# Graph layer with residual and layer norm: a ring of 24 chunks instead of 84, and one 192-wide sum per chunk instead of one 496-wide sum per three chunks

## What is computed

```
h_self   = x @ W_self.T + b_self
messages = x[src] @ W_neigh.T + b_neigh
h_neigh  = segment_sum(messages, dst, 50000)
y        = x + relu(h_self + h_neigh)
out      = (y - mean(y)) / sqrt(var(y) + 1e-5)      # per node
```

## Time and profile before

| | us |
|---|---|
| median of 3 runs (lowest to highest) | 804.39 (798.32 to 804.57) |
| the profiled execution | 803.84 |
| its span, first to last instruction | 802.0 |
| busy: PE / DVE / ACT / POOL | 557.8 / 446.4 / 303.2 / 403.5 |

### The profile page before, as it was taken

The page is one execution under the profiler, slowest core; times in us unless marked ns, Lnnn a source line. Parts: engine busy times, 40 slices in busy tenths (PEclk is TensorE's granted clock), DMA queues, the critical chain, the costliest instruction groups (busy, mean ns, idle before and its releaser), DMA issues. The chain is left out here.

```text
span 802.0 us, 11397 instructions
## 1 busy us (share of the span) xinstructions
PE 557.8 (70%) x3151; PEld 441.7 (55%) x3151; DVE 446.4 (56%) x1927; ACT 303.2 (38%) x789; POOL 403.5 (50%) x424
## 2 busy tenths in 40 slices
PE   2054011069742979888678886978897988999995
PEld 0033001048631767666557675756675776778784
DVE  8880100048812777776566757565554555566765
ACT  0000000025311535444234544535453544566566
POOL 5777777520375656660756666556565666100000
PEclk9998555559955989998879999889997999999998
DMA  2421211123312434453334443444444444433433
GB/s 76 120 56 52 62 52 52 43 60 101 104 52 63 127 113 128 132 150 95 102 93 134 123 133 110 123 114 132 115 136 112 131 123 134 119 105 101 116 104 93
DMA packets 122933, 82.12 MB, mean 102 GB/s; under 512 B 15374, under 2 KB 115894, under 8 KB 122840
## 3 DMA queue, kind: packets, MB, share of 16 engines
q1 hardware_dynamic: 109208, 53.63, 23.7%
q0 software_dynamic: 13664, 27.77, 12.9%
HBM read 55.44 MB, written 26.71 MB: 102 GB/s over the span
## 5 line engine op out<-in xcount | busy, mean ns | idle before, releaser
L467 POOL DMA_INDIRECT ring<-in_x,chunk_src x391 | 378.7, 968 | 271.7 <-issue 110.9
L994 ACT COPY sums_t<-bank 128x496 f32 x131 | 74.8, 571 | 423.9 <-remote 202.2
L893 PE MATMUL bank<-pick,ring 128*128 128x192 f32 (+2 forms) x782 | 231.9, 437 | 4.0 <-DMA ring<-in_x,chunk_src 4.0
L739 DVE SCALAR_TENSOR_TENSOR y<-bank,x_in 128x384 f32<-128x384 f32 x131 | 72.6, 554 | 215.7 <-remote 173.2
L912 PE MATMUL bank<-wsum_t,x_t 128*128 128x128 f32 (+1 forms) x782 | 175.4, 307 | 15.2 <-issue 15.2
L913 PE MATMUL bank<-wn_t,sums_t 128*128 128x128 f32 (+1 forms) x782 | 160.8, 287 | 24.2 <-issue 24.2
L1021 ACT ACTIVATE result<-y,minus_mean,rstd 128x128 f32<-128x128 f32 x391 | 163.4, 486 | 0.0
L893 PEld LDWEIGHTS bank<-pick,ring 128*128 128x128 f32 x782 | 146.1, 210 | 19.0 <-issue 4.3
L912 PEld LDWEIGHTS bank<-wsum_t,x_t 128*128 128x128 f32 (+1 forms) x782 | 126.6, 203 | 40.0 <-issue 39.8
L913 PEld LDWEIGHTS bank<-wn_t,sums_t 128*128 128x128 f32 (+1 forms) x782 | 127.6, 204 | 24.8 <-issue 24.8
L887 PE MATMUL bank<-carry,ring 128*128 128x1 f32 x260 | 44.6, 241 | 106.8 <-DVE pick L728 77.8
(11 more groups left out here) (122 smaller groups left out, 207.9 us busy)
## 6 DMA issues: line engine op xcount, KB each, us to landing
x_in<-in_x SPq DMA_DIRECT2D x130, 192.0 KB
out<-result SPq DMA_DIRECT2D x130, 192.0 KB
ring<-in_x,chunk_src POOLq DMA_INDIRECT x391
degrees_t<-degrees_dram SPq DMA_DIRECT2D x130, 2.2 KB
dst_padded<-in_dst SPq DMA_DIRECT2D x1, 390.6 KB
src_padded<-in_src SPq DMA_DIRECT2D x1, 390.6 KB
edge_src<-in_src SPq DMA_DIRECT2D x1, 390.6 KB
edge_dst<-in_dst SPq DMA_DIRECT2D x1, 390.6 KB
```

The lines of the kernel that those rows point to most:

```text
L467: nc.gpsimd.indirect_dma_start(ring[:, c % RING, :], None, x, bass.IndirectOffsetOnAxis(ap=chunk_src[:, c:c + 1], axis=0)).then_inc(gather ...
L739: v.scalar_tensor_tensor(y[tau % DEEP][0:rows, 0:tiles, :], h_bank[b][0:rows, 0:tiles * DIM].rearrange("p (q d) -> p q d", q=tiles), 0.0, ...
L893: ins = mm(sums[:, lo:hi], ring[:, c % RING, :], pick[tau % DEEP][:, PICK_AT[q]:PICK_AT[q] + hi - lo], start=(tau == 0 and q == 0), stop=( ...
L994: nc.scalar.copy(sums_t[:, bass.ds(at, SPAN)], sum_bank[tau % SUM_BANKS][:, 0:SPAN]).then_inc(sums_placed, 1)
```

## The change

Two things are changed at once.

**The ring** has 24 slots instead of 84, and POOL waits for each chunk by itself (`chunks_summed`) and no longer for triples.

**The sums** are made chunk by chunk. Each chunk covers 192 columns counted from its own first node; two chunks stand side by side in one bank, at columns 0 and 192. The pick of the first of a pair is 193 columns wide: its last column adds the edges that belong to the second's first node. The second's own overhang goes into column 0 of the next pair's bank by a `carry` matmul, so there is one carry matmul for two chunks. ACT copies 192 columns per chunk, each copy waiting for the one before, with one wait on the sums for a pair. Registers are loaded eight at a time. There are four sum banks, and one bank for the turned `x`. The margin that is joined at a lap's end is 192 columns wide instead of 512, and the drift allowed is 640 nodes instead of 768 (384 within 42 chunks of either end, 192 within 9). How far the sums run ahead is now counted in chunks: what is needed, plus 2, rounded up to a whole pair.

```diff
-SPANS = ((0, 192), (64, 344), (168, 496))
-SPAN = SPANS[-1][1]
-PICK_AT = (0, 192, 472)
-PICK = 800
+SPAN = 192
+PAIR = 2
...
-MARGIN = 512
+MARGIN = SPAN
-DRIFT = 768
+DRIFT = 640
...
-RING = 84
+RING = 24
-SUM_BANKS = 3
-LOAD = 4
+SUM_BANKS = 4
+LOAD = 8
...
+def chunks_starting_below(node):
+    return 1 + max(c for c in range(CHUNKS) if P * c - drift_of(c) < node)
+def whole_pairs(chunks):
+    return min(CHUNKS, -(-chunks // PAIR) * PAIR)
 def sums_needed(trio):
-    return 1 + max(c for c in range(TRIOS) if P * TRIO * c - drift_of(c) < P * TRIO * (trio + 1))
+    return chunks_starting_below(P * TRIO * (trio + 1))
+def sums_ahead(trio):
+    return whole_pairs(sums_needed(min(trio, TRIOS - 1)) + PAIR)
...
                 if c >= RING:
-                    pool.wait_ge(triples_summed, (c - RING) // TRIO + 2)
+                    pool.wait_ge(chunks_summed, c - RING + 1)
...
-    dve.wait_ge(triples_summed, tau - DEEP + 1)
+    dve.wait_ge(chunks_summed, TRIO * (tau - DEEP + 1))
-    ins = v.tensor_scalar(pick[tau % DEEP][:, PICK_AT[q]:PICK_AT[q] + hi - lo], columns[:, lo:hi],
-                          local[:, c:c + 1], None, ALU.is_equal)
+    ins = v.tensor_scalar(pick[tau % DEEP][:, c % TRIO, :], columns[:], local[:, c:c + 1], None, ALU.is_equal)
...
-                if tau >= 2:
-                    pe.wait_ge(xt_copied, tau - 1)
+                if tau >= 1:
+                    pe.wait_ge(xt_copied, tau)
...
+            def sum_chunk(c):
+                tau = c // TRIO
+                if c % TRIO == 0:
+                    pe.wait_ge(pick_built, tau + 1)
+                    pe.wait_ge(gathered[tau % GATHER_SEMS], gathers_upto(tau))
+                frame = SPAN * (c % PAIR)
+                into = sum_bank[c // PAIR % SUM_BANKS]
+                carried = 1 - c % PAIR
+                ins = mm(into[:, frame:frame + SPAN + carried], ring[:, c % RING, :], pick[tau % DEEP][:, c % TRIO, 0:SPAN + carried],
+                         start=(c == 0), stop=True, skip_group_check=True)
+                if c % PAIR == 1:
+                    if c // PAIR + 1 >= SUM_BANKS:
+                        pe.wait_ge(sums_placed, PAIR * (c // PAIR + 2 - SUM_BANKS))
+                    ins = mm(sum_bank[(c // PAIR + 1) % SUM_BANKS][:, 0:1], ring[:, c % RING, :], carry[:, c:c + 1], start=True, stop=False, skip_group_check=True)
+                ins.then_inc(chunks_summed, 1)
...
+            def place_sums(c):
+                if c % LOAD == 0:
+                    load_offsets(c)
+                at = act.snap(held[c % LOAD], min_val=0, max_val=LAP - 1)
+                if c % PAIR == 0:
+                    act.wait_ge(chunks_summed, min(c + PAIR, CHUNKS))
...
+                    act.wait_ge(sums_placed, c)
...
+                frame = SPAN * (c % PAIR)
+                nc.scalar.copy(sums_t[:, bass.ds(at, SPAN)], sum_bank[c // PAIR % SUM_BANKS][:, frame:frame + SPAN]).then_inc(sums_placed, 1)
```

More of the change, by code:

```diff
@@ L235, in build_common_case @@
     degrees = sb("degrees", [SPREAD, COLUMNS, P], BF16)
[L238 removed]
+    expected = sb("expected", [1, CHUNKS])
     gap = sb("gap", [1, CHUNKS])
[L240 removed]
+    faults = sb("faults", [1, 8])
     unused = sb("unused", [1, CHUNKS])
[L244 removed]
+    columns = sb("columns", [P, SPAN + 2])
     ring = sb("ring", [P, RING, DIM])
     x_in = [sb(f"x_in{i}", [P, TRIO, DIM]) for i in range(DEEP)]
[L247 removed]
+    pick = [sb(f"pick{i}", [P, TRIO, SPAN + 2]) for i in range(DEEP)]
     sums_t = sb("sums_t", [P, LAP + MARGIN])
@@ L843, in _ @@
                     clear_lap(cleared_at[t - 1])
-                while built < min(TRIOS, sums_needed(min(t + 1, TRIOS - 1)) + 1):
+                while built * TRIO < sums_ahead(t + 1):
                     build_picks(built)
@@ L878, in turn_x @@
                 ins.then_inc(xt_turned, 1)
-            def sum_chunks(tau):
-                sums = sum_bank[tau % SUM_BANKS]
-                pe.wait_ge(pick_built, tau + 1)
-                if tau >= SUM_BANKS:
-                    pe.wait_ge(sums_placed, tau - SUM_BANKS + 1)
-                if tau:
-                    mm(sums[:, 0:1], ring[:, (tau * TRIO - 1) % RING, :], carry[:, tau - 1:tau], start=True, stop=False, skip_group_check=True)
-                pe.wait_ge(gathered[tau % GATHER_SEMS], gathers_upto(tau))
-                chunks = chunks_of(tau)
-                for c in chunks:
-                    q = c % TRIO
-                    lo, hi = SPANS[q]
-                    ins = mm(sums[:, lo:hi], ring[:, c % RING, :], pick[tau % DEEP][:, PICK_AT[q]:PICK_AT[q] + hi - lo],
-                             start=(tau == 0 and q == 0), stop=(c == chunks[-1]), skip_group_check=True)
-                ins.then_inc(triples_summed, 1)
+            def sum_chunk(c):
[13 more added lines that the diff above has]
+                ins.then_inc(chunks_summed, 1)
@@ L949, in _ @@
                 later_lists(t)
-                while summed < min(TRIOS, sums_needed(t) + 1):
-                    sum_chunks(summed)
+                while summed < sums_ahead(t):
+                    sum_chunk(summed)
                     summed += 1
```

111 lines of the change are left out of this document (46 added, 65 removed).

## The result

The changed kernel takes **699.17 us** (693.77 to 704.63, 4 runs), beside 804.48 us (798.32 to 807.9) for the kernel before on the same chip: a ratio of **0.868**, 95% interval 0.860 to 0.876. Some executions of a kernel fall in a slower state of the chip; medians here are of all executions, ratios and intervals of the undisturbed ones alone. The forecast was 714 in a range of 640 to 790. The trace that follows is of the fastest execution, 693.77 us; the trace of before is of one of 803.84.

What follows compares the result with a forecast made beforehand. It took PE's updates, late while POOL gathers without a gap, as the bound: 88 us start + 127 triples x 4.78 (4.85 - 0.17 + 0.10) = 695, plus 17.5 end and 1.8 around the span: 714 us, range 640 to 790.

Steps and rivals of the forecast that it cites:

- The lag: PE's semaphore updates reach VectorE and ScalarE late, 34 and 54 us, while POOL gathers without a gap; 3.1 us with the ring full.
- the early stall: First run of gathers: 93 back to back before; with 24 slots, 32 ending at 78 us, pipeline flowing at 88 us.
- the list waits: POOL's waits for the second and third lists, 52.8 us of its idle time before, were to go.
- The pace: Time per triple with gathers and PE both running: 4.78 us over 127 triples; 4.4 to 5.2 had chance 0.6.
- two small terms: Corrections to the base pace per triple: 0.17 us less for narrower sums, 0.10 us more for the copies' later place.
- the mixed pace: Full-ring pace of the kernel before, 4.95 us for 56 triples with list work, 4.77 for 71; mean 4.85 a triple.
- The narrower sums: PE's sum matmuls cover 577 columns per triple instead of 800; 0.17 us less a triple was taken.
- The tight copy: In odd iterations PE's products need a chunk summed and copied by ScalarE in that iteration; cost 0.10 us a triple.
- slower, through the tight copy: Rival: PE waits each odd iteration for ScalarE's copy while the short ring stops POOL; pace 5.63, 822 us, chance 0.09.
- The end: From the last triple but one or two to the end of the span, 17.5 us.
- runs of 5 or 6 gathers with pauses of 2 us: Sign of a right forecast: POOL makes 5 to 6 gathers in a row, then pauses 2 us.
- The better rival: Gathers broken up so well that the lag hardly builds: pace 3.8 to 4.4, 628 us (590 to 666), chance 0.2.

## Why the prediction was right, and where it was off

**The lag and the early stall** were right, in kind and in size. The forecast had 32 gathers and a stop at 78 us; it was 33 and 81.5. It had the pipeline flowing at 88; chunk 18 was summed at 95.91, where the forecast, with four triples at 88, would have had 88 + 2 x 4.78 = 97.6. The second stall, for which the forecast wrote only that the list waits and their long runs would go, was worth 35 us. That the lag is caused by the gathers, which the rows of before only suggested, the runs with two gathers of three show. By what mechanism is not shown by any run, nor whether the update is held up or the matmul itself: a matmul's end is modelled here, and in the starved stretch of before PE's own matmuls stand apart without a wait that the profile shows:

```profile
99.20 0.59 PE L887 MATMUL bank<-carry,ring 128*128 128x1 f32 x2 [22.33 <-issue]
```

One thing more is in the trace of the changed kernel. Of the 131 updates that follow a triple's products, 87 come more than 0.5 us late while gathers go on, and 65 of these fall into a pause of POOL, 0.59 to 1.48 us after a gather's end. That fits updates which pass when the gathers pause. It doesn't prove it, since POOL's pauses themselves end with updates of PE.

**The pace** was forecast at 4.78 and measured at 4.72 (4.77 from the 21st residual to the 101st), but its terms fared less well, and that it came so near is luck: a base 0.05 too high made up for two small terms that together came to 0.03 less instead of 0.07. The 4.85 of the mixed pace with the long-ring form of the sums was 4.80 with 24 slots. The narrower sums were to bring 0.17 and brought about nothing (4.77 against 4.80). The work did shrink: 170.04 us of L889 over 717 records, six a triple, are 1.42 us a triple, but this is far from the forecast's 1.15, which started from the 1.59 of the stretch without gathers; beside gathers the kernel before took 99.58 / 58 = 1.72. The clock was 0.87 in this window, where the ring-full stretch of before had 0.94.

**The tight copy** was to cost 0.10 a triple. Its mechanism is in the trace:

```profile
440.12 0.75 ACT L996 COPY sums_t<-bank 128x192 f32 x2 [0.99 <-remote]
...
440.58 0.47 PE L908 MATMUL bank<-bias,degrees_t 12*128 12x384 bf16 x1 [2.12 <-issue]
...
440.98 0.79 PE L912 MATMUL bank<-wsum_t,x_t 128*128 128x128 f32 x2
...
445.37 0.49 PE L912 MATMUL bank<-wsum_t,x_t 128*128 128x128 f32 x2
...
450.50 0.75 ACT L996 COPY sums_t<-bank 128x192 f32 x2 [2.07 <-remote]
450.66 0.94 POOL L482 DMA_INDIRECT ring<-in_x,chunk_src  x1 [1.16 <-remote]
...
450.96 0.47 PE L908 MATMUL bank<-bias,degrees_t 12*128 12x384 bf16 x1 [1.95 <-issue]
```

PE stands idle for 1.95 us ahead of L908 at 450.96, and the copy for which it waits starts at 450.50, after 2.07 us of waiting for a late update; the same happened at 440.58. After such a pause the granted clock is down: 0.50, the lower of its two levels (1.2 of 2.4 GHz), in the 3 us behind 440.6, and 1.00 from 445.1 on, where no pause came before. The first pair of L912 takes 0.79 us in the one stretch and 0.49 in the other:

```profile
440.60:443.60 3.00, 3.00 (x13) 2.66 (x14) 0.64 (x7) 2.62 (x8) 2.16 (x3) 0.50 0.50 133
445.10:446.70 1.60, 1.60 (x13) 1.42 (x13) 0.92 (x4) 0.63 (x3) 0.64 (x1) 1.00 0.22 56
```

PE's waits ahead of L908 in the two rows above are 41.4 + 9.6 = 51.0 us, **0.39 a triple**, and nearly all end right behind a copy of the sums, where the kernel before with 24 slots waited for its picks instead:

```profile
PE bank L887 <- DVE pick L728: 65.8, 35, 4.6
```

That is 65.8 us, 0.50 a triple. So the sums per chunk moved PE's wait from the picks to the copy of the sums, and what they took off PE's work was lost to a lower clock. Between 100 and 650 us, with 24 slots, first with sums per triple and then per chunk:

```profile
100.00:650.00 550.00, 466.53 (x2756) 372.13 (x2755) 357.21 (x1568) 264.04 (x690) 337.96 (x343) 0.94 0.47 126
```

```profile
100.00:650.00 550.00, 463.54 (x2901) 411.32 (x2899) 340.32 (x1582) 309.84 (x928) 335.93 (x347) 0.87 0.46 128
```

The clock is 0.94 and 0.87, though PE stands idle about as long, 83.5 and 86.5 us. Why the pauses of the one kernel cost more clock than those of the other is open. The sum matmuls fell from 274.6 to 221.3 us over all, while the products, the same instructions, rose from 169.8 + 154.7 = 324.5 to 361.9, which is 0.29 a triple. The rival "slower, through the tight copy" had the right place, and by these totals its price was wrong because PE would have waited about as long elsewhere.

**The end** was mis-sized: 3 triples at 4.78 and 17.5, 31.8 us in all, stood in the forecast after chunk 384, and it took 692.0 - 671.52 = 20.5. The last triples run without gathers, which the text said and the sum left out. This is 11 of the 21 us by which the profiled span missed the sum of 712; the pace over 122 triples is 8, the start 2.

**Right as told:** the list waits are gone; the copies of 192 columns take 319 ns (335 forecast); ScalarE was busy 2.65 us a triple, from 321.71 us (just under the 2.7 to 3.2 forecast); POOL ended 37 us before the span; the gathers' median stayed at 944 ns beside VectorE's picks. **Wrong:** runs of 5 or 6 gathers with pauses of 2 us. POOL went 2 to 4 gathers at a time, with pauses of about 1 us. And the bound of the pace was misread. I set it down as two parties that wait for each other, and looked for the cure in their waits; the run with two gathers of three says that it goes with the number of gathers. The better rival (pace 3.8 to 4.4) asked for gathers broken up by a ring; in the changed kernel they come 2 to 4 at a time and with 6 slots never more than 6, and the pace is 4.72 and 4.67.

## What to carry to other kernels

A deep buffer in front of a prefetching engine is not free: where the prefetch disturbs its consumer, its length can set how long the disturbance lasts before the consumer's progress is asked for. Look for an engine that runs without a pause while all others wait for events long past, and try a short ring before anything else; here one constant was worth 14% (84 to 12 slots in the kernel before). And where no engine is busy all the time, leave out a fixed share of one kind of instruction and time the rest: leaving out 130 gathers gave back 1.14 us for each, which no table of busy time had said.

## What the runs showed of the hardware

- While GpSimd issued indirect DMAs of 128 rows one after the other (0.944 us and 0.30 between), semaphore updates of TensorE reached VectorE and ScalarE 34 and 54 us behind the modelled ends of its matmuls, at a DMA share of 0.18.
- With 1.44 us from one gather to the next and no other pause, the longest wait for such an update was 8.4 us; with a full ring of 12 slots it was 3.4.
- The update behind a triple's last product came a median of 0.81 us after that matmul's modelled end with three gathers a triple and 24 slots, 0.11 with two, and 0.01 with two and a memset.
- With two gathers a triple PE ran at a clock of 0.98 and 3.68 us a triple; with three the pace was 4.7 to 4.8 whatever the ring from 48 slots down. Half the rows or half the bytes in each changed nothing.
- A gather of 64 rows took GpSimd 908 ns, one of 128 rows 944.
- A GpSimd memset of 128 x 2200 fp32 took 1.95 us, one of 128 x 128 0.23, and three picks on VectorE of which the first began with the long one took 2.57 us instead of 0.77. All 111 picks that overlapped a memset ended 0.12 us after it, whichever record began first.
